# Mixture of experts: the first block's rows of expert weights spread by TensorE, the table's clearing and cast at other places

## The reference, cut to what matters

```python
logits = x2d @ gate_w.T
rw = softmax(logits)
_, sel = top_k(sigmoid(logits), 4)
w = take_along_axis(rw, sel); w = w / w.sum(-1)
cw_large = zeros(T, 32).at[rows, sel].add(w)
cw_small = zeros(T, 16).at[rows, sel // 2].add(w)
# for each expert e, with 96 (large) or 128 (small) inner rows:
a = silu(x @ Wg[e]) * (x @ Wu[e]) * cw[:, e]
y += a @ Wd[e]            # small experts times 0.05
...
w = lut[idx]              # the last layer's weights, lut of 16 values
```

## Time and profile before

| | |
|---|---|
| time, median of 3 runs | 1070.91 us (1070.79 to 1071.02) |
| the profiled execution | 1069.07 us, span 1067.3 us |
| mean granted TensorE clock | 0.953 |
| TensorE busy | 945.4 us (89%) |
| VectorE busy | 853.8 us (80%) |
| GpSimd busy | 690.5 us (65%) |
| ScalarE busy | 561.4 us (53%) |

### The profile page before, as it was taken

How to read it: one execution, slowest core, us unless ns; L and a number is a source line. 1 busy time by engine, 2 the same in 40 slices (tenths; PEclk the granted TensorE clock), 3 DMA queues, 4 the chain that set the end, 5 groups by cost and what they waited for, 6 DMA issues and landing times. The chain is left out here.

```text
span 1067.3 us, 13034 instructions
## 1 busy us (share of the span) xinstructions
PE 945.4 (89%) x3804; PEld 593.5 (56%) x3804; DVE 853.8 (80%) x1117; ACT 561.4 (53%) x1128; POOL 690.5 (65%) x382
## 2 busy tenths in 40 slices
PE   5898867999999999996969897999989997777798
PEld 2566646888888888884524432443434342222587
DVE  3688777778777777776658899899988999999853
ACT  2688742333333333332766777775776667564141
POOL 3388624555565565552269998899989999999000
PEclk9899988999999999998979999899989998989899
DMA  3000025342442452322155656566555655664001
GB/s 95 1 2 0 1 115 174 108 138 83 124 138 69 120 155 69 109 68 72 33 136 146 155 181 167 127 155 175 157 137 147 164 147 161 154 168 121 0 1 40
DMA packets 60031, 115.04 MB, mean 108 GB/s; under 512 B 10400, under 2 KB 15776, under 8 KB 59856
## 3 DMA queue, kind: packets, MB, share of 16 engines
q1 hardware_dynamic: 58848, 112.61, 38.3%
q10 hardware_dynamic: 1136, 1.90, 0.6%
HBM read 112.98 MB, written 1.51 MB: 107 GB/s over the span
## 5 line engine op out<-in xcount | busy, mean ns | idle before, releaser
L1733 POOL TENSOR_TENSOR uB<-u,rows_B 128x1024 f32<-128x1024 f32 x127 | 298.6, 2363 | 0.0
L872 POOL TENSOR_TENSOR lutw<-lutw,lt 128x865 f32<-128x865 f32 x80 | 184.7, 2309 | 164.3 <-DVE lt L838 158.6
L1972 PE MATMUL ya<-hV,ident 128*128 128x512 f32 x320 | 179.7, 649 | 48.3 <-DVE hV L1852 41.0
L1952 DVE TENSOR_TENSOR_SCAN da<-da,uB 128x512 f32<-128x512 f32 x160 | 193.9, 1224 | 14.5 <-ACT da L1837 13.5
L1743 POOL TENSOR_TENSOR hP<-hS,rows_C 128x512 f32<-128x512 f32 x96 | 122.3, 1274 | 26.6 <-PE ya L1972 14.9
L1972 PEld LDWEIGHTS ya<-hV,ident 128*128 128x128 f32 x320 | 58.3, 199 | 138.7 <-DVE hV L1852 90.2
L1949 DVE TENSOR_TENSOR_SCAN hS<-da,uB 128x512 f32<-128x512 f32 x96 | 116.3, 1212 | 14.4 <-ACT da L1837 9.0
L746 ACT ACTIVATE ah<-ups 128x1024 fp32r<-128x1024 f32 x40 | 41.2, 1029 | 129.9 <-DVE ups L834 129.9
L1852 DVE TENSOR_TENSOR hV<-da,rows_C 128x512 f32<-128x512 f32 x160 | 107.5, 672 | 0.0
L1972 PE MATMUL ya<-hP,ident 128*128 128x512 f32 x192 | 102.2, 614 | 0.0
L831 DVE TENSOR_TENSOR si<-gps,cwb 128x1024 f32<-128x1024 f32 x40 | 49.0, 1225 | 56.7 <-ACT gps L743 53.1
(11 more groups left out here) (357 smaller groups left out, 2014.3 us busy)
## 6 DMA issues: line engine op xcount, KB each, us to landing
rows_B<-bc_rows SPq DMA_DIRECT2D x128, 256.0 KB, 3.7
rows_C<-bc_rows SPq DMA_DIRECT2D x128, 256.0 KB, 4.4
wr<-in_moe_w SPq DMA_DIRECT2D x40, 384.0 KB, 4.6
cwb<-cw_rows SPq DMA_DIRECT2D x16, 512.0 KB, 4.1
cwb<-cw_rows SPq DMA_DIRECT2D x16, 384.0 KB, 4.6
cwb<-cw_rows SPq DMA_DIRECT2D x16, 256.0 KB, 3.9
lut_f<-in_lut_idx SPq DMA_DIRECT2D x1, 2160.0 KB, 9.0
cwb<-cw_rows SPq DMA_DIRECT2D x16, 128.0 KB, 4.1
```

What stands on the lines that cost most here:

```text
L872: e.tensor_tensor(part, part, lt[:, q, :], ALU.add).then_inc(s_la, 1)
L1733: e.tensor_tensor(uB[:, r % UPAIRS, :, :], u[:, d:d + 2, :], RB[:, r % BROWS, :].unsqueeze(1).broadcast_to([P, 2, HALF]), ALU.mult).then_i ...
L1952: e.tensor_tensor_scan(a[:, way], a[:, way], uB[:, r % UPAIRS, b, way], 0.0, ALU.mult, ALU.add).then_inc(s_sc, 1)
L1972: return e.matmul(ya[n % 2][:, :], g.ident[:, :], at, start=False, stop=False, skip_group_check=True).then_inc(done, 1)
```

## The change

Three things are done at other places or in another way.

The first block's `cwb` doesn't come through memory. GpSimd makes a selector `sel`, whose rows 0 and 1 tell which of the 128 partitions belong to expert 0 (the first 96) and to expert 1; TensorE multiplies it by the first two rows of `cwT`, half by half, into the second bank of `yps`; ScalarE and VectorE copy a half each into `cwb`. The up rows of block 0 come after this on TensorE, and the matmuls by zero, which clear the same bank, after the first `si`. ScalarE does the SiLU of block 0 ahead of its copy of `cwT`. The first round of blocks is written out ahead of the loop, which runs over six rounds. The table `cwT` still goes to memory for the other blocks.

The sums `lutw` are cleared when both halves of `xl` are done. The indices are cast behind block 0's `ups * si`.

```diff
@@ SP
-            e.wait_ge(s_te, NH)
+            e.wait_ge(s_te, 1)
+            e.wait_ge(s_tg, 1)
             e.dma_start(dram["cw"], cwT[:, :]).then_inc(cw_out, 16)
...
                     e.wait_ge(s_tc, START + (n - 1 if k >= 2 else n - 2))
-                    if k < 3:
+                    if isinstance(n, int) and n == 0:
+                        pass
+                    elif k < 3:
...
-            with e.Fori(0, MOE_IT - 1) as j:
+            blocks(0)
+            with e.Fori(1, MOE_IT - 1) as j:
@@ ScalarE
             e.preload_act_table_set("silu_and_others")
+            e.wait_ge(s_g, START + 1)
+            e.activation(gps[:, :], gps[:, :], ACT.Silu).then_inc(s_si, 1)
             e.wait_ge(s_ct, 1)
             e.activation(cwT[:, half(0)], ctps[:, half(0)], ACT.Copy).then_inc(s_te, 1)
+            e.wait_ge(s_cb, 1)
+            e.activation(cwb[:, ESLOT[0], half(0)], cbps[:, half(0)], ACT.Copy).then_inc(s_cc, 1)
@@ VectorE
-            e.tensor_copy(cwT[:, half(1)], ctps[:, half(1)]).then_inc(s_te, 1)
-            e.wait_ge(lut_in, 16)
-            e.tensor_copy(g.lut_f[:, 0:LUTW], lut_i[:, 0:LUTW]).then_inc(s_lf, 1)
-            e.wait_ge(s_lf, 1)
+            e.tensor_copy(cwT[:, half(1)], ctps[:, half(1)]).then_inc(s_tg, 1)
+            e.wait_ge(s_cb, NH)
+            e.tensor_copy(cwb[:, ESLOT[0], half(1)], cbps[:, half(1)]).then_inc(s_cc, 1)
...
-                    e.wait_ge(s_c[k], (j + 1) * (32 if k < 3 else 16))
+                    if isinstance(n, int) and n == 0:
+                        e.wait_ge(s_cc, NH)
+                    else:
+                        e.wait_ge(s_c[k], (j + (0 if k == 0 else 1)) * (32 if k < 3 else 16))
...
                     e.tensor_tensor(ups[:, :], ups[:, :], si[:, s, :], ALU.mult).then_inc(s_a, 1)
 
+                    if isinstance(n, int) and n == 0:
+                        e.wait_ge(lut_in, 16)
+                        e.tensor_copy(g.lut_f[:, 0:LUTW], lut_i[:, 0:LUTW]).then_inc(s_lf, 1)
+                        e.wait_ge(s_lf, 1)
                     e.wait_ge(s_la, START + 2 * n)
@@ GpSimd
             e.memset(ah[:, ZA, :].bitcast(F32), 0.0).then_inc(s_z, 1)
+            e.tensor_copy(sel[:, 0:INTER], g.ident[:, 0:1].broadcast_to([P, INTER])).then_inc(s_sel, 1)
+            e.tensor_copy(sel[:, INTER:], g.ident[:, 1:2].broadcast_to([P, P - INTER])).then_inc(s_sel, 1)
+
+            e.wait_ge(s_lo, KC)
             e.memset(g.lutw[:, :], 0.0).then_inc(s_z, 1)
@@ TensorE
+            e.wait_ge(s_sel, 2)
+            e.wait_ge(s_wo, 2)
+            for h in range(NH):
+                e.wait_ge((s_te, s_tg)[h], 1)
+                e.matmul(cbps[:, half(h)], sel[0:2, :], cwT[0:2, half(h)], start=True, stop=True).then_inc(s_cb, 1)
             rows(ups, 0, 1, s_u)
 
             e.wait_ge(s_z, 2)
-            e.wait_ge(s_te, NH)
-            e.wait_ge(s_wo, 2)
+            e.wait_ge(s_tc, START + 1)
```

More of the change, by code:

```diff
@@ L620, in experts @@
         sem, [f"rt_{n}" for n in "gh gl lg lt lT pad le m8 mr sh ex me sm rc cw pr ct te".split()])
-    s_1d, s_gw, s_of, s_wp, s_wo = map(sem, [f"rt_{n}" for n in "1d gw of wp wo".split()])
+    s_1d, s_gw, s_of, s_wp, s_wo, s_sel, s_cb, s_cc, s_tg = map(sem, [f"rt_{n}" for n in "1d gw of wp wo sel cb cc tg".split()])
     s_w = [sem(f"ex_w{k}") for k in range(MOE_K)]
@@ L638, in experts @@
     cwb = c.sb(ctx, "cwb", [P, 3, T])
+    sel = c.sb(ctx, "cw_sel", [P, P])
     si = c.sb(ctx, "si", [P, 3, T])
@@ L662, in experts @@
     ctps, wps = yps[0:NCW, 0, :], yps[:, 1, 0:2 * D].rearrange("p (a d) -> p a d", a=2)
+    cbps = yps[:, 1, :]
     def half(h):
@@ L741, in blocks @@
                         split_high(e, (k + 1) % K, j * 16 + (16 if k < K - 1 else 32))
-                    e.wait_ge(s_g, START + n + 1)
-                    e.activation(gps[:, :], gps[:, :], ACT.Silu).then_inc(s_si, 1)
+                    if not isinstance(n, int) or n:
+                        e.wait_ge(s_g, START + n + 1)
+                        e.activation(gps[:, :], gps[:, :], ACT.Silu).then_inc(s_si, 1)
                     e.wait_ge(s_d, START + n + 1)
```

## The result

The changed kernel is 0.39% faster in the first comparison: ratio to the kernel before 0.9961, 95% interval [0.9945, 0.9977]; 1064.61 us median against 1070.19. Compared again later (ten runs of the changed kernel), the ratio is 0.9977 [0.9960, 0.9994]; 1065.29 against 1068.10. The forecast, 1067.9 against 1070.91, is a ratio of 0.9972 and lies between the two. So the ratio came true, but the trace shows that two errors met in it.

What follows compares the result with a forecast made beforehand. TensorE's unbroken run bounds the experts' stage, so its start at 172.05 us decides. Clearing 2.58 plus spread 2.15 minus clock 1.7 gives 3.0 us: 1067.9 us against 1070.91, own range 1066.7 to 1069.1, 8 in 10 within 1065.9 to 1069.7.

Steps and rivals of the forecast that it cites:

- The clearing: Stage's head: with the memset behind the second `xl`, line 770 falls from 2.75 to 0.17 us; 2.58 us gained.
- MAX8 was not held: Router: MAX8 beside the moved memset could start 0 to 1.0 us late; 0 taken. Being held belonged to rival 2, chance 0.17.
- The spread's matmuls and `si`: Block 0: two fp32 matmuls of 0.88 us each; `si` from 162.35 on the old clock in place of 166.28.
- With 12 matmuls 0.23 apart they are ready at 163.4: Block 0's up rows on TensorE, after the spread, ready just before `ups * si` at 163.6 on the old clock.
- 2.58 + 2.15 = 4.7: Gain at TensorE's second-block up rows: 2.58 us from the clearing, 2.15 from those rows starting at 169.9 instead of 172.05.
- The cast: VectorE, behind block 0's `ups * si`: no longer covered by the wait for rows, it costs its whole 2.6 us before `al`.
- The rest for `al` and the fall behind it: TensorE rests some 2.5 us before the second block's up rows; its clock falls, eight matmuls run slow, 1.7 us lost.
- Rival 1: TensorE's clock does not fall in the 2.5 us rest, or the rest is shorter: 4.7 us gained, 1066.2; chance 0.15.
- the row that the forecast took for its fall: A TensorE rest of 2.41 us before 539.66, followed by four fp32 records in 3.65 us, some 0.88 apart instead of 0.44.
- The sum inside the stage: Experts' stage: 2.58 + 2.15 - 1.7 = 3.0 us gained.
- so the end of the kernel moves too: The stage ends with a barrier of all engines, so moving its end moves the kernel's end by as much.
- The code written out again: The five first blocks written out cost nothing; rival 4 had 1.1 us lost in each, 1073.4, chance 0.05.

Runs made afterwards that it cites:

- Before's other two profiles: Profiles of the kernel before with one and with two idle VectorE copies before the stage's barrier; stage 361.96 and 361.31 us with the copies taken off.
- the two profiles that reach it together: Changed kernel with the clearing put back in its old place (ratio 0.9958), and changed kernel with two idle copies before the barrier (0.9988).
- The delays: Idle 1024-column VectorE copies before the stage's barrier: kernel before, one 0.9978, two 1.0020; changed kernel, two 0.9988; 48-row spread plus cast in the wait, one 0.9926.

## Why the prediction was right or wrong

The time was right as a ratio, the working only in part, and that the two errors nearly cancelled was luck.

- **The clearing**: 2.58 us forecast. The normalisation stands 2.74 us behind the stage's first aggregate, where it stood 5.33 (142.52 - 137.19): 2.59. Alone it gave 2.7. Right, and MAX8 was not held: it starts 12.54 us behind the aggregate against 15.17 before, 2.63 less, in the middle of the memset. That the memset held the tiny operation is shown both ways: 0.17 us with the memset moved alone, 2.75 us with it put back. The first half of the Trainium skill's rule (GPSIMD Engine Reference, table of the specifications), on VectorE's two-port modes, fits this, though no view shows the mode. The second half, on two SBUF inputs, did not apply here: the subtraction behind MAX8, which has two, began at 151.15, 0.2 us before the memset ended, and was not held. A memset reads nothing, however. Beside GpSimd's additions, which read SBUF (169.57 to 174.34 in before), VectorE's `wl`, with two SBUF inputs, took 1.67 us at 171.09 where it took 0.96 at 161.66.
- **The spread's matmuls and `si`**: `si` forecast at 162.35 - 2.58 = 159.8, or 22.6 us behind the first aggregate; measured 160.07 - 137.70 = 22.4. Right. The four records took 1.95 us with 2 rows and with 48: the rows of the contraction cost no time.
- **"With 12 matmuls 0.23 apart they are ready at 163.4"**: this step failed. At the fallen clock they were 0.43 apart, and the product started 1.9 us after the end of `si`. The working had the clock fall only in pauses, not behind a busy stretch of small contractions. TensorE took up the second block's up rows 172.05 - 137.19 = 34.9 us behind the first aggregate before, and 169.34 - 137.70 = 31.6 after: 3.2 us gained where 2.58 + 2.15 = 4.7 was forecast. So this term is 1.5 us too large, which is what the spread over 48 rows gives back (1.4 us). Before's other two profiles have 35.9 and 35.2 us here, and against their mean with the first the gain is 3.7 us.
- **The cast**: 2.6 us forecast in front of `al`. It is 2.44 from its start to the compares, and the kernel with the cast in the wait is 3.9 us shorter in the stage, cast and clock together. Right in direction and size; what was not seen is that a 1.60 us wait for the spread's matmuls lay idle in front of it. Put there, the cast makes `si` only 0.7 us later.
- **The rest for `al` and the fall behind it**: 2.5 us forecast, 2.60 measured; 1.7 us of loss forecast, and 3.2 - 1.7 = 1.5 measured, as the difference between what TensorE had gained at the up rows and what the stage had gained at its end. Right. Rival 1, no fall, is out, and with it what the Trainium skill (TensorE: Matmul & The Clock Gate, section Why this matters for your kernels), which warns only of longer gaps, would have made of this one. But the row that the forecast took for its fall could have misled elsewhere: in the scans of the changed kernel a rest of 2.65 us, in front of 647.86, is followed by a pair at full clock (1.12 us), and so it is in four other profiles. The length of a rest alone does not tell.
- **The sum inside the stage**: 3.0 forecast, 1.7 measured between the first two profiles, 2.1 between the means. The step "so the end of the kernel moves too", that is, later stages follow, failed as well, by 2.7 us the other way in the profiled run. The forecast gave the later stages 1.2 us to either side; one low stretch in the scans, with what follows from it, moves them by 3.2 us (the two profiles that reach it together). The two errors nearly cancelled, which is why 1067.9 looks better than it was.
- **The code written out again** cost nothing: behind the head, TensorE waits in the stage only for the 1.1 us at its very end, as before.

What stays open: why one execution of the same kernel meets the stretch and another does not. The delays show that moving the scans by a microsecond or two changes the whole time by more than the move. But two profiles that reach the place 0.02 us apart differ in it, so the move alone is not the cause, and a shift is no sure way to the gain. What sets the timing of the clock's changes, and why the changed kernel escapes only in some of its runs, is not shown here.

## What to carry to other kernels

A wait that you remove gives back only what the next engine in line can use: look at every idle gap around the new chain, since work pushed out of the old wait may fit in the new one (here 3.9 us by moving one cast). In this kernel, with pauses of 1 to 3 us on TensorE, an idle copy of 1.2 us took 2.2 us off the whole time. So measure a stage inside the trace, in more than one profile (before's own stage differed by 1.1 us), and test a small whole-time gain with a pure delay before believing its cause.

## What the runs showed of the hardware

TensorE's clock fell to 1.2 GHz during steady work: behind four fp32 records over 2 rows in 1.95 us and a pause of 0.3 us, in five profiles of five (in one of them 1 us into the next matmuls), and in none of three with 48 rows at the same length and pause. Where between 2 and 48 rows this changes was not tried.

The same pauses, 1.35 and 1.70 us with a pair of 1.12 us between them, were followed by 1.2 GHz in five of twelve profiles and by the full clock in seven, even at the same place in the span (613.10 and 613.12 us). A rest of 2.60 us in the changed kernel was followed by the fall, one of 2.65 us later in the same profile was not. A copy of 1.2 us in front made a kernel of 1070 us 2.2 us faster.
